# VectorE's half of the ring work moves behind the next minima, and the finishing steps are spread over twice as many half steps

## What is computed

```python
Q, K, V = xq @ Wq + bq, xkv @ Wk + bk, xkv @ Wv + bv      # 16 heads of 16 (a6: 8 heads of 32)
s = Q @ K.T / sqrt(dk);  s = where(mask or causal, -inf, s)
out = softmax(s) @ V                                       # (4 batches, 512 x 512 scores per head)
x = layernorm(x + out @ Wo + bo) * g + b                   # a0, a1, a6: no Wo; a2, a3: no layernorm
```

## Time and profile before

| | |
|---|---|
| median of the runs | 3414.09 us |
| the profiled execution's own time | 3420.81 us |
| its span, first to last instruction | 3419.0 us |
| TensorE matmul, busy | 3026.8 us (89%) |
| VectorE, busy | 1914.5 us (56%) |
| ScalarE, busy | 1492.1 us (44%) |
| mean granted TensorE clock | 0.93 |

### The profile page before, as it was taken

One profiled execution on the slowest core, in us unless ns is written; L12 is line 12 of the kernel. 1 busy time (PEld: TensorE's weight loads), 2 busy tenths in 40 slices (PEclk: granted clock), 3 DMA queues, 4 the chain that ended last, 5 costly groups with the idle time before them and its releaser, 6 DMA issues. The chain is left out here.

```text
span 3419.0 us, 47618 instructions
## 1 busy us (share of the span) xinstructions
PE 3026.8 (89%) x17126; PEld 1808.1 (53%) x17248; DVE 1914.5 (56%) x4677; ACT 1492.1 (44%) x2134; POOL 451.8 (13%) x538
## 2 busy tenths in 40 slices
PE   6888888856999999989999999996999999978686
PEld 3444333342444444379898989993444444347353
DVE  4666777654767776443333333334777777734354
ACT  1333444521555555544444444431555555543233
POOL 0111111143211111010000000001122221113112
PEclk7889888976999999989999999997999999998798
DMA  4212121103222222000000000003222222100331
GB/s 116 49 40 57 46 64 46 30 1 70 76 61 82 67 77 60 18 25 26 26 25 26 26 26 26 1 1 69 78 61 87 58 76 58 30 1 1 83 86 49
DMA packets 75113, 162.66 MB, mean 48 GB/s; under 512 B 15401, under 2 KB 21673, under 8 KB 72697
## 3 DMA queue, kind: packets, MB, share of 16 engines
q1 hardware_dynamic: 74872, 159.51, 17.8%
HBM read 60.76 MB, written 2.10 MB: 18 GB/s over the span
## 5 line engine op out<-in xcount | busy, mean ns | idle before, releaser
L883 ACT ACTIVATE probT_a<-scores 128x1024 f32<-128x1024 f32 (+3 forms) x832 | 785.1, 949 | 841.8 <-PE scores L737 469.8
L992 DVE CUSTOM_DVE_ANT_0 ring<-ring,maskb_a 128x512 f32<-128x512 f32 x1024 | 681.9, 719 | 204.8 <-PE ring L754 175.1
L754 PE MATMUL ring<-stacks_a 64*128 64x512 f32 (+7 forms) x1664 | 451.9, 422 | 72.2 <-DMA stacks_a<-fixed_a 26.0
L1329 DVE TENSOR_TENSOR hidden_moe<-whole_moe,hidden_moe 128x512 fp32r<-128x512 f32 x288 | 199.8, 694 | 519.9 <-ACT whole_moe L1251 519.7
L775 PE MATMUL outputs<-probT_a,V_a 128*32 128x512 f32 (+6 forms) x3328 | 451.1, 586 | 23.9 <-ACT probT_a L883 11.8
L1172 PE MATMUL scores<-tokens_moe,weights_moe 128*128 128x512 f32 x1728 | 447.8, 395 | 4.9 <-issue 4.9
L719 PE MATMUL scores<-stacks_a 64*128 64x512 f32 (+7 forms) x1664 | 415.6, 480 | 0.0
L719 PEld LDWEIGHTS scores<-stacks_a 64*128 64x128 f32 (+1 forms) x1664 | 166.4, 188 | 464.0 <-issue 344.9
L990 DVE TENSOR_REDUCE negm_a<-ring 128x1 f32<-128x512 f32 (+3 forms) x640 | 329.7, 562 | 144.5 <-PE ring L760 103.2
L1185 PE MATMUL ring<-weights_moe,hidden_moe 128*128 128x256 f32 x2592 | 402.8, 283 | 4.0 <-DVE hidden_moe L1329 3.4
L1185 PEld LDWEIGHTS ring<-weights_moe,hidden_moe 128*128 128x128 f32 x2592 | 367.6, 191 | 30.7 <-issue 4.6
(11 more groups left out here) (151 smaller groups left out, 3240.7 us busy)
## 6 DMA issues: line engine op xcount, KB each, us to landing
stacks_a<-parts_a SPq DMA_DIRECT2D x672, 128.0 KB
raw<-in_moew SPq DMA_DIRECT2D x9, 2048.0 KB, 7.5
maski_a<-in_mask SPq DMA_DIRECT2D x16, 1024.0 KB, 5.3
wt<-in_w SPq DMA_DIRECT2D x7, 1024.0 KB, 5.0
kvT_a<-in_ctxT SPq DMA_DIRECT2D x12, 512.0 KB, 3.5
stacks_a<-fixed_a SPq DMA_DIRECT2D x4, 1024.0 KB
wrow<-in_row SPq DMA_DIRECT2D x7, 512.0 KB, 6.2
stacks_a<-mrow_a SPq DMA_DIRECT2D x224, 8.0 KB
```

The costliest lines, as they stand in the source:

```text
L754: last = pe.matmul(bank("S", j, n, e)[:, 0:w], Q[rows, g, qt * P:(qt + 1) * P], K[rows, g, 0:w], start=True, stop=not a.causal)
L883: act.activation(probT[:, kb % 2, 2 * p:2 * p + 2, q0:S], scores_bank(j, n)[:, :, q0:S], ACT.Exp, bias=0.0, scale=-1.0).then_inc(c_exp.sem, 1)
L992: least = dve.tensor_tensor_reduce(sc, sc, maskb[:, m % 2, qt, :], 1.0, BIG * 2, ALU.add, ALU.min, out)
L1329: dve.tensor_tensor(hidden[:, m % 4, 1, :], whole[:, m % 2, :], hidden[:, m % 4, 0, :].bitcast(F32), ALU.subtract).then_inc(c_low.sem, 1)
```

## The change

`late` names the items whose read-out is VectorE's. TensorE's and ScalarE's part of such an item stay where they are. VectorE's part gets a name of its own (`"q_late"` and so on). If the item is the last ring user of its half step, the late part is put off into the next half step, behind its `S` and `exp`. If not, it stays at its place. The count `c_rD`, for which TensorE waits, is now kept in the new order. In `timetable`, `ot`, `y` and `ln` move to later half steps, and `rinv` gets a second buffer.

```diff
     for qt in range(QT):
-        out += [(2 + qt, "on", -1, qt), (3 + qt, "ot", -1, qt), (4 + qt, "y", -1, qt),
-                (qt + (5 if a.wo else 3), "ln", -1, qt)]
+        out += [(2 + qt, "on", -1, qt), (4 + qt, "ot", -1, qt), (6 + qt, "y", -1, qt),
+                (qt + (8 if a.wo else 4), "ln", -1, qt)]
...
+    put_off = []
...
             if there(j):
                 yield ("exp", j, h)
+            for kind, k, n in put_off:
+                yield (kind + LATE, k, n)
+            put_off.clear()
+            now = []
...
+            rings = [i for i, item in enumerate(now) if item[0] in RINGED]
+            for i, (work, k, n) in enumerate(now):
+                yield (work, k, n)
+                if work in RINGED and work != "m" and late(work, n, ATT[int(units[k - base][0][1:])]):
+
+                    if i == rings[-1]:
+                        put_off.append((work, k, n))
+                    else:
+                        yield (work + LATE, k, n)
...
+def late(work, n, a):
+    return work in ("q", "k", "on", "y") or (work in "xc" and n == 1) or (work == "V" and a.bias)
...
-        rinv = sb("rinv", [P, heads, 1], F32)
+        rinv = sb("rinv", [P, 2, heads, 1], F32)
...
         for given, key in turns:
             c_ring.mark(*key)
-            given.mark(*key)
+            if given is c_rA:
+                given.mark(*key)
+        for kind, j, n in work:
+            if kind == "S":
+                for e in range(2):
+                    c_rD.mark("S", j, n, e)
+            elif kind.endswith(LATE):
+                c_rD.mark(kind[:-len(LATE)], j, n)
+            elif kind in RINGED and turns[ring[kind, j, n]][0] is c_rD and not late(kind, n, stage_of(j)[2]):
+                c_rD.mark(kind, j, n)
...
-                if kind in ("q", "k"):
-                    col = n + (KB if kind == "k" else 0)
+                if kind in ("q" + LATE, "k" + LATE):
+                    of = kind[0]
+                    col = n + (KB if of == "k" else 0)
```

More of the change, by code:

```diff
@@ L191, in schedule @@
                     if there(4 * m + n):
-                        yield (work, 4 * m + n, 0)
+                        now.append((work, 4 * m + n, 0))
                     continue
@@ L197, in schedule @@
                     if wanted(work, ATT[int(st[1:])], st, b, st == stages[0]):
-                        yield (work, k, n)
+                        now.append((work, k, n))
+            rings = [i for i, item in enumerate(now) if item[0] in RINGED]
[6 more added lines that the diff above has]
+                        yield (work + LATE, k, n)
             kb = h // couples - 1
@@ L204, in schedule @@
                     yield ("PV", j - 1, QT - 1)
+LATE = "_late"
+def late(work, n, a):
+    return work in ("q", "k", "on", "y") or (work in "xc" and n == 1) or (work == "V" and a.bias)
 RINGED = {"x": "AD", "c": "AD", "q": "DD", "k": "DD", "V": "AA", "len": "DD", "m": "AA", "on": "DDDD",
@@ L449, in attention_block, with stage_of @@
         work = list(schedule(stages, base))
+        def stage_of(m):
+            st, b = units[m]
+            return st, b, att[st], int(st[1:]) % 2
         ring, turns = {}, []
@@ L528, in halves_before @@
             return divmod(j * halves + h - n, halves)
-        def stage_of(m):
-            st, b = units[m]
-            return st, b, att[st], int(st[1:]) % 2
         @block.sync
@@ L1003, in _ @@
                                              op1=ALU.subtract).then_inc(c_split.sem, 1)
-                if kind not in ("tokens", "norms", "x", "c", "q", "k", "V", "len", "on", "y", "ln"):
+                if kind not in ("tokens", "norms", "len", "ln") and not kind.endswith(LATE):
                     continue
@@ L1019, in _ @@
                     dve.tensor_scalar(ms[:, :], ss[:, :], 1.0 / D, 1e-5, ALU.mult, ALU.add).then_inc(c_sums.sem, 1)
-                if kind == "x" and n == 1:
+                if kind == "x" + LATE:
                     dve.wait_ge(*c_ring.at("x", j, 1))
@@ L1027, in _ @@
                         dve.tensor_copy(xT[:, 1, :], bank("x", j, 1)[:, :]).then_inc(c_rD.sem, 1)
-                if kind == "c" and n == 1:
+                if kind == "c" + LATE:
                     dve.wait_ge(*c_ring.at("c", j, 1))
                     dve.tensor_copy(kvT[:, 1, :], bank("c", j, 1)[:, :]).then_inc(c_rD.sem, 1)
-                if kind in ("q", "k"):
-                    col = n + (KB if kind == "k" else 0)
-                    if n == 0 and kind == "q":
+                if kind in ("q" + LATE, "k" + LATE):
+                    of = kind[0]
+                    col = n + (KB if of == "k" else 0)
+                    if n == 0 and of == "q":
                         dve.wait_ge(c_ready, which + 1)
-                    dve.wait_ge(*c_hi.at(kind, j, n))
+                    dve.wait_ge(*c_hi.at(of, j, n))
                     dve.scalar_tensor_tensor(
-                        out=parts[:, n, low[kind], :], in0=bank(kind, j, n)[:, :],
-                        scalar=wcol[:, k, col:col + 1], in1=parts[:, n, high[kind], :].bitcast(F32),
+                        out=parts[:, n, low[of], :], in0=bank(of, j, n)[:, :],
+                        scalar=wcol[:, k, col:col + 1], in1=parts[:, n, high[of], :].bitcast(F32),
                         op0=ALU.add, op1=ALU.subtract).then_inc(c_rD.sem, 1)
-                if kind == "V" and a.bias:
+                if kind == "V" + LATE:
                     if j == base and n == 0:
@@ L1050, in _ @@
                     lengths(j, n)
-                if kind == "on":
+                if kind == "on" + LATE:
                     view = bank("on", j, n)[:, :].rearrange("p (h s) -> p h s", s=slot)
                     dve.wait_ge(*c_ring.at("on", j, n))
-                    dve.reciprocal(rinv[:, :, :], view[:, :, a.dk:a.dk + 1])
+                    dve.reciprocal(rinv[:, n % 2, :, :], view[:, :, a.dk:a.dk + 1])
                     dve.drain()
                     if a.length:
-                        dve.tensor_scalar(rinv[:, :, :], rinv[:, :, :], keep[:, which, b * QT + n:b * QT + n + 1],
+                        dve.tensor_scalar(rinv[:, n % 2, :, :], rinv[:, n % 2, :, :], keep[:, which, b * QT + n:b * QT + n + 1],
                                           None, ALU.mult)
@@ L1062, in _ @@
                     dve.tensor_tensor(o[:, n % 2, :].rearrange("p (h s) -> p h s", s=a.dk), view[:, :, 0:a.dk],
-                                      rinv[:, :, :].to_broadcast([P, heads, a.dk]), ALU.mult).then_inc(c_rD.sem, 1)
+                                      rinv[:, n % 2, :, :].to_broadcast([P, heads, a.dk]), ALU.mult).then_inc(c_rD.sem, 1)
                     if not a.wo:
@@ L1067, in _ @@
                         moments_of(j, n)
-                if kind == "y":
+                if kind == "y" + LATE:
                     dve.wait_ge(*c_ring.at("y", j, n))
```

## The result

The changed kernel takes 3787.68 us (median of four runs, 3781.88 to 3790.37), the kernel before 3413.32 us beside it. The ratio is 1.1093, with a 95% interval of 1.1077 to 1.1109: 374 us slower. The forecast was 278 slower. The sign and the main mechanism held. The time lies outside the 3620 to 3760 of the forecast's own case and only 2 us inside the upper end of the wider range. 96 us were missing: 45 came from a place that I had not thought of, the put-off cost some 23 more than forecast, and the spread gave back 29 less.

The account below looks back on a forecast made before the run. TensorE was taken as the bound (89% busy), paying in full for held banks. Added: a2/a3 106, a4/a5 91, a0/a1 57, a6 24, together 278 us, rounded to 3690 us, 8% slower; 3580 to 3790 holds 8 in 10.

Parts of the forecast that it names:

- the forecast's own case: Whole kernel: 3620 to 3760 us, chance 0.70, with plain waits of 1.2 to 1.8 us.
- the wider range: Whole kernel: 3580 to 3790 us, 8 in 10, with parts of the absorbed and falling-clock cases.
- the 0.6 us of old waits: Finishing steps of a2/a3: existing waits, such as 0.33 us before `on` 1, about 0.6 together, set against the new ones.
- A held bank stops TensorE: All blocks: TensorE waits for banks held by put-off read-outs, 0.5 to 1.9 us at projections, about 2.0 at finishing steps.
- 20.0 and 9.0 forecast: Half steps 3 to 9 in a2: 19.99 us before, net 9.0 us more per unit from finishing-step bank waits.
- The clock there stays near 1.00: Sign of being right: in a2/a3 the granted clock holds; under 0.95 in a2 to a5 would mean a larger part missed.
- the rival with 0.13: New waits in a2 to a5 lower TensorE's clock: 8 us more in 14 units, +112 us, 3800; chance 0.13.
- The argument against it: Against a falling clock: new waits are under 2 us, and half step 9 in a4 waits longer at block clock 0.99.
- the 3.4 us: a4/a5, half step 9: 6.85 us against 3.50 in a2, a loss put down to VectorE falling behind on layernorms.
- the 6.85 us: Half step 9 of a4/a5, with 1.53 us in front of `m`; forecast to shrink to about 6.
- Spreading the steps should give this back: a4/a5 finishing steps: layernorm chains spread over seven half steps return 4.1 us per unit, leaving net 4.9 of 9.0.
- In a0/a1 VectorE is the bound in these half steps already: a0/a1 finishing steps: VectorE busy 16.66 of 20 us, so only 1.3 us more per unit, one extra idle start.

Follow-up runs that it names:

- experiment 3: Changed kernel with GpSimd's mask step at half step 13 instead of 10: 3742.58 us, ratio 1.0959 to the kernel before.
- 4: Changed kernel with nothing put off (new timetable kept) and the mask step at half step 13: 3405.08 us, ratio 0.9970 to the kernel before.
- experiment 1: Changed kernel with nothing put off, so the new timetable alone, mask step still at half step 10: 3446.98 us, ratio 1.0101 to the kernel before.
- 7: Control: the kernel before, old timetable, with only the mask step moved from half step 10 to 13: 3418.02 us, ratio 1.0002.
- experiments 4 to 6: Changed kernel, nothing put off: new timetable, mask step at 13 (0.9970) or 12 (0.9971); in-between timetables, mask step at 10 (0.9960; `ot` earlier 0.9978).

## Why the prediction was right or wrong

Blocks in us over the kernel before, in the profiled executions (369 us apart). "Put-off" is experiment 3 against 4, the same timetable and mask step with and without it; the third column is what the prediction's terms give without what the spread was to return (4.1 us per unit) and the 0.6 us of old waits.

| block | changed kernel | predicted | put-off, predicted | put-off, measured |
|---|---|---|---|---|
| a0/a1 | 82 | 57 | 57 | 95 |
| a2/a3 | 114 | 106 | 110 | 111 |
| a4/a5 | 137 | 91 | 124 | 84 |
| a6 | 27 | 24 | 24 | 32 |
| outside the blocks | 8 | - | - | 14 |

**A held bank stops TensorE: right, shown.** The wait stands in front of the forecast items and at the forecast places, and it goes when nothing is put off (experiment 1). Sizes, from the half steps of a2 and a4 in most units:

| put off, next user | predicted | half step before, after | measured |
|---|---|---|---|
| `k` 1, to `S` of 14 | 1.5 | 2.34, 3.60 | 1.26 |
| `q` 0, to `S` of 30 | 1.5 | 4.06, 5.32 | 1.26 |
| `k` 0, to `S` of the next 0 | 1.5 | 2.34, 3.69 | 1.35 |
| `q` 1, to `S` of 11 | 0.5 | 1.20, 1.60 | 0.40 |
| `x` 1, to `m` of 25 | 1.9 | 1.64, 3.38 | 1.74 |
| `V` 0, to `mT` 1 of 18 (a4) | 1.9 | 2.42, 4.10 | 1.68 |

After `x` 1 half step 26 gives 0.35 back. The finishing half steps 3 to 9 of a2 take 28.0 us at full clock (20.0 and 9.0 forecast, 29.0).

**"The clock there stays near 1.00": wrong.** It was the rival with 0.13, and it came in part: 0.95 and 0.94 for the two middle blocks (in a4/a5 mostly through the hole of half step 13: 0.98 with the mask step at 13). Against the same half steps at full clock, half steps 4 to 7 cost 20 us more in a2/a3 and 11 in a4/a5. That is well short of the 112 us of the rival. The argument against it, that half step 9 in a4 waited longer at 0.99 for the block, misread a mean: that very half step ran at 0.75 (experiment 4). So of the 3.4 us that I put down to VectorE falling behind there, 1.5 were the clock. The forecast that the 6.85 us would shrink to about 6 came true by this: 5.92 us at 1.00, where the same at 1.00 was 5.4 before. In a2/a3 it made up for terms that were a little too large, which is why that block seems to fit. The Trainium skill ("TensorE: Matmul & The Clock Gate", section "A second HAM failure mode: psum-queue depth-cycling") tells of a clock that swings because TensorE idles briefly between groups of matmuls as it cycles PSUM banks. By that the clock would swing here; the trace agrees in nine of the half steps 4 and 6 of a2/a3 (0.50 to 0.75) and not in the other five (1.00).

**The step that failed: "Spreading the steps should give this back", with nothing said of GpSimd's queue.** I costed the moved `ln` on VectorE and TensorE only, and returned 4.1 us per unit in a4/a5. In fact the last `ln` moved past `maskcv` in GpSimd's queue, and the return became a loss of 45 us (experiments 1, 3, 4, 7). Its 7 us stand in the page's group of GpSimd, and `ln` begins with GpSimd's `rstd`, so both could be read before. The return itself was too large as well: 15 us in half steps 3 to 9 of a4/a5 rather than 29, and about 9 of them at equal clock. Part of it went where `y` 2 and `y` 3 came to stand, in half steps 8 and 9 (experiment 4). What the spread did return came where the sum had nothing: 11 us in a0/a1 and 4.5 in a6, from the `ln` alone.

**"In a0/a1 VectorE is the bound in these half steps already", 1.3 us per unit: mis-sized.** With only the finishing steps put off, a0/a1 grow by 39 us over experiment 1 (16 in a0, 23 in a1), 5.6 us for each of seven units, where I had 9 us in all. TensorE's loads in a1, half steps 3 and 4:

```profile
534.72 0.57 PEld L887 LDWEIGHTS ring<-identf,oT_a 128*128 128x128 f32 x4 [2.79 <-DVE o_a L1094]
...
539.19 0.71 PEld L887 LDWEIGHTS ring<-identf,oT_a 128*128 128x128 f32 x4 [3.07 <-DVE o_a L1094]
```

and what VectorE does meanwhile:

```profile
535.75 0.18 DVE L998 BATCH_NORM_AGGREGATE mv<-bn 128x2 f32<-128x6 f32 x1
536.87 1.29 DVE L1021 TENSOR_REDUCE negm_a<-ring 128x1 f32<-128x512 f32 x2 [0.94 <-PE ring L785]
538.08 0.25 DVE L1086 RECIPROCAL rinv_a<-ring 128x16 f32<-128x16 f32 x1
```

VectorE waits 0.94 us for the scores, TensorE then 3.07 us for VectorE, and it was so in the half step before (2.79): they take turns, where before VectorE's `on` overlapped TensorE's next scores. I had counted that idle time once per unit; it comes in each half step that has an `on` before it. In a0, three units show it in half step 3 at a clock of 1.00 either way: 1.26 us in experiment 1, 3.13 with the finishing steps put off. A high busy share over 20 us didn't mean that VectorE always had work at hand. The clock has a share in it too. Half step 4 of a unit of a0, first in experiment 1, then with the finishing steps put off:

```profile
143.00:146.20 3.20, 2.83 (x21) 1.35 (x20) 2.79 (x10) 1.09 (x2) 0.76 (x2) 1.00 0.01 2
148.60:153.90 5.30, 3.38 (x21) 1.44 (x20) 3.80 (x11) 0.60 (x1) 1.49 (x3) 0.60 0.00 0
```

With these put-offs half step 4 runs at 0.50 to 0.77 in all seven units. How much of the 39 us is the turns and how much the clock, no run separates. The projections' share there, 59 us, was also above the 48 of the forecast.

**In a4/a5 the put-off cost less than forecast (84 for 124)**, because half step 16, which waits 11 us for the mask in experiment 4, no longer does where the put-offs have made the half steps before it longer, and because the finishing half steps 3 to 9 lost 7.4 us per unit, not 9.6.

**The sum.** 374 us: 338 for the put-off, 45 for the mask step, 8 returned by the spread. Predicted: 315, 0 and 37. That the put-off came within 23 us of its forecast is in part luck: by block it is 38 us over in a0/a1, 8 in a6 and 14 outside the blocks, and 40 under in a4/a5.

## What to carry to other kernels

A read-out that frees a bank is part of the path of whoever takes the bank next; with a ring of three of which two go to every step, putting it behind the next step's work makes TensorE wait for that work too (here 1.3 to 1.7 us each time), even if VectorE was idle before it. When a multi-engine item moves in a list, walk its move through every queue it has a part in, the least busy ones too: one long instruction on an idle engine (here 7 us on GpSimd at 12% busy) is enough. And run the pieces on their own: the spread alone looked like a small loss (1.0101), but without the collision with the mask step it is a gain of 0.2 to 0.4% (experiments 4 to 6), and by blocks that gain is not where it was looked for. Last, read the clock of the very half step, not that of its block: a wait that seems to be an engine's can be the clock's.

## What the runs showed of the hardware

The granted clock fell to 0.50 to 0.52 for single half steps of 6.5 to 7.6 us in a block whose other half steps run at 1.00 for the most part, after waits of 2.04 to 2.07 us each with matmuls between, and came back within the same unit (1.00 in the 42.9 us from half step 10 to 27 of the unit shown, of which TensorE was busy for 39.27):

```profile
1241.40:1284.30 42.90, 39.27 (x230) 16.46 (x234) 27.61 (x78) 24.54 (x30) 2.93 (x2) 1.00 0.21 52
```

The same waits in other units of the block left it at 1.00. It also differs between executions: half step 9 of a4/a5 ran at 0.75 to 0.79 in four of six units of the kernel before and at 1.00 in all six of the control of 7, which has the same timetable but for the mask step. The weight loads show it too: those of `ST` take 0.19 us at full clock and 0.29 at the start of the half steps at 0.52 and 0.50.
